# Attention steps of a two-layer decoder: the second scores of a key tile are issued ahead of the values of the tile before

## The reference: what is computed

```
w = jnp.einsum('bhnd,bhmd->bhnm', q, k) * jax.lax.rsqrt(float(D))
w = jnp.where(mask > 0, w, NEG)        # causal layers only
w = jax.nn.softmax(w, axis=-1)
attn = jnp.einsum('bhnm,bhmd->bhnd', w, v)
```

## Time and profile before

| | |
|---|---|
| median of 3 runs | 2826.07 us (2823.96 to 2826.38) |
| the profiled execution | 2821.3 us, its span 2819.5 us |
| PE busy | 2510.2 us, 89% |
| PE weight loads | 1440.7 us, 51% |
| DVE busy | 1492.1 us, 53% |
| ACT busy | 1328.4 us, 47% |
| POOL busy | 445.9 us, 16% |
| mean granted TensorE clock | 0.952 of full speed |
| context groups, 423 to 705 us | PE 266.5 us of 282, DVE 231.8, ACT 192.1, clock 0.99 |
| context groups, 1676 to 1930 us | PE 245.5 us of 254, DVE 206.5, ACT 175.1, clock 1.00 |

### The profile page before, as it was taken

One profiled execution on the slowest core, in us unless ns is written; L12 is line 12 of the kernel. 1 busy time (PEld: TensorE's weight loads), 2 busy tenths in 40 slices (PEclk: granted clock), 3 DMA queues, 4 the chain that ended last, 5 costly groups with the idle time before them and its releaser, 6 DMA issues. The chain is left out here.

```text
span 2819.5 us, 47227 instructions
## 1 busy us (share of the span) xinstructions
PE 2510.2 (89%) x15793; PEld 1440.7 (51%) x15794; DVE 1492.1 (53%) x4176; ACT 1328.4 (47%) x2833; POOL 445.9 (16%) x687
## 2 busy tenths in 40 slices
PE   6999999899979889998799999999998993599991
PEld 3555544444434456675466544444445653377661
DVE  2555877788544500023555688877746654222224
ACT  2655466667744422111355557666665551122220
POOL 4233221101100000000123312212023001400004
PEclk8999999999989999999799999999999995699996
DMA  7545533233000022113644543242223318201103
GB/s 222 162 142 144 139 98 94 53 80 79 1 1 0 1 95 95 63 49 120 196 128 141 144 98 94 53 116 71 66 86 98 101 44 292 96 30 33 33 30 95
DMA packets 153825, 259.89 MB, mean 92 GB/s; under 512 B 22713, under 2 KB 96705, under 8 KB 149441
## 3 DMA queue, kind: packets, MB, share of 16 engines
q1 hardware_dynamic: 150544, 248.81, 30.9%
q0 software_dynamic: 3072, 8.39, 0.9%
HBM read 180.71 MB, written 81.53 MB: 93 GB/s over the span
## 5 line engine op out<-in xcount | busy, mean ns | idle before, releaser
L1449 ACT ACTIVATE second_p<-psum 128x512 f32<-128x512 f32 (+3 forms) x1024 | 461.1, 522 | 234.7 <-PE psum L1291 231.2
L1449 ACT ACTIVATE first_p<-psum 128x512 f32<-128x512 f32 (+3 forms) x768 | 366.6, 548 | 164.2 <-PE psum L1291 160.8
L1541 DVE TENSOR_REDUCE second_max_parts<-psum 128x1 f32<-128x512 f32 x512 | 322.6, 683 | 67.6 <-PE psum L1268 65.5
L1541 DVE TENSOR_REDUCE first_max_parts<-psum 128x1 f32<-128x512 f32 x512 | 322.6, 683 | 63.3 <-PE psum L1268 61.0
L1537 DVE CUSTOM_DVE_ANT_0 second_masked<-psum,mask_qk 128x384 f32<-128x384 f32 (+3 forms) x512 | 229.4, 488 | 180.9 <-PE psum L1268 160.5
L1303 PE MATMUL psum<-second_p,second_v_aug 128*32 128x512 f32 (+3 forms) x2048 | 232.8, 527 | 6.0 <-ACT second_p L1449 4.8
L1268 PE MATMUL psum<-second_k,second_q 64*128 64x512 f32 (+3 forms) x1024 | 199.4, 386 | 28.3 <-DMA second_k<-a_k_parts 14.3
L1281 PE MATMUL psum<-second_q,second_k 64*128 64x512 f32 (+3 forms) x1024 | 222.1, 430 | 2.5 <-ACT second_shift_T L1460 0.7
L1291 PE MATMUL psum<-second_shift_T,choose 64*128 64x512 f32 (+3 forms) x1024 | 194.9, 376 | 0.0
L1281 PEld LDWEIGHTS psum<-second_q,second_k 64*128 64x128 f32 x1024 | 96.6, 184 | 182.1 <-ACT second_p L1449 76.5
L1303 PE MATMUL psum<-first_p,first_v_aug 128*32 128x512 f32 (+3 forms) x1536 | 184.9, 554 | 1.1 <-ACT first_p L1449 0.7
(11 more groups left out here) (337 smaller groups left out, 3867.5 us busy)
## 6 DMA issues: line engine op xcount, KB each, us to landing
first_k<-c_k_parts SPq DMA_DIRECT2D x64, 256.0 KB
second_q<-a_q_parts SPq DMA_DIRECT2D x128, 128.0 KB, 2.9
second_k<-a_k_parts SPq DMA_DIRECT2D x128, 128.0 KB, 2.9
second_k<-c_k_parts SPq DMA_DIRECT2D x64, 256.0 KB, 4.5
first_q<-a_q_parts SPq DMA_DIRECT2D x64, 128.0 KB
first_k<-a_k_parts SPq DMA_DIRECT2D x64, 128.0 KB
c_k_parts<-first_held SPq DMA_DIRECT2D x16, 512.0 KB, 3.1
first_q<-c_q_parts SPq DMA_DIRECT2D x64, 128.0 KB
```

What stands on the lines that cost most here:

```text
L1449: evacuated(act.activation(probs[tile % 2][:, 2 * h + p, q0:SEQ], bank[:, q0:SEQ], ACT.Exp, scale=scale), event)
L1541: evacuated(v.reduce_max(max_parts[n % 2][:, h, p, qt, k0 // BANK:k0 // BANK + 1], bank[:, 0:width], axis=AX_X), event)
```

## The change

The event scores (t,1), with the shift ahead of it in the last step, moves from behind the values, the turn and the loads to directly behind the first unit. The last two groups of each stage, which had it so already, stay as they are.

```diff
             share(units, 2 * t + 1, 2 * steps)
+            if n + 2 < groups:
+                if t == steps - 1:
+                    plan.append(("shift", n + 1, 0))
+                plan.append(("scores", n, (t, 1)))
             if t:
                 plan.append(("values", n, t - 1))
             elif n:
...
                 if n + 3 < groups:
                     plan.append(("vload", n + 3, 0))
-            if n + 2 < groups:
-                if t == steps - 1:
-                    plan.append(("shift", n + 1, 0))
-                plan.append(("scores", n, (t, 1)))
             share(units, 2 * t + 2, 2 * steps)
```

## The result

The changed kernel takes 2865.93 us (median of 4 runs, 2863.12 to 2869.14) against 2826.23 (4 runs, 2823.96 to 2830.89): 1.0137 times the time before, interval 1.0122 to 1.0152. It is slower by 39.7 us. The forecast was 2836, slower by 10.5, range 2812 to 2853. The direction was right, and so was the wait named as the one that takes the place of the removed one. The size was not, and a part that had been put at nothing, the steps with pieces, was not nothing. One of the twelve executions of the kernel with one-unit groups only took 6053.3 us and is left out of its ratio; every other execution in this document lies within 0.3% of its kernel's median.

What follows compares the result with a forecast made beforehand. ACT's latency loop binds plain context steps (2.94 us), DVE close behind. Terms -1 + 6.5 + 6 + 4 + 1 - 6 = +10.5 take the profiled 2821.3 to 2832, 2836 on the median's scale; range 2812 to 2853.

Steps and rivals of the forecast that it cites:

- Wait removed: Context steps: values stop waiting for ACT's second exponential, the first unit for the first; 0.34 us per plain step was waiting.
- Wait that takes its place: Plain context steps: second scores wait for DVE's maximum of the unit behind values; 2.93 against 2.94, 117 steps, -1 us.
- Turn: 25 context steps with the turn: the unit's maximum queues behind DVE's normalising multiply; +0.26 each, +6.5 us.
- shift: 23 context steps with the shift: second scores wait for both banks of the unit before; +0.26 each, +6 us.
- one unit: 10 steps with a single unit: no unit stands behind values, so DVE's wait can't arise; -0.6 each, -6 us.
- DVE's other work: 8 context groups with outputs: chain and statistics beyond DVE's spare 0.46 a step reach PE; 0 to +8, taken as +4 us.
- Causal groups without pieces: 12 groups: ACT-bound steps gain 2 x 0.34, the shift's wait for the chain loses 0.76; +1 us, bounds -8 to +9.
- Steps with pieces ...: 0: Steps with pieces (PE the bound), and groups 14 and 15 with four units a step (DVE the bound): no change, 0.
- the free wait: Rival, chance 0.12: DVE frees the bank by the time PE comes, all 0.34 a step is gained; 2764 us.
- weights loaded ahead: Rival, chance 0.08: the unit behind values starts as quickly as any, 0.12 x 165 = 20 less than forecast; 2816 us.
- plain exchange: Rival, chance 0.22: normalisation and double bank wait in turn and shift steps are hidden; -6, 2820 us.
- DVE becomes the bound: Rival, chance 0.18: in steps 0 to 2 and beside own pieces DVE's work passes 2.93 a step; +14, 2850 us.

Runs made afterwards that it cites:

- the kernel with one-unit groups only: Against the kernel before: second scores ahead of values only in the two groups whose steps have one unit; 2822.59 us, ratio 0.998.
- scores in pairs: Against the kernel before: in context groups both scores of a step in a row, then unit, values, unit; 2802.53 us, ratio 0.9904.
- The last step as before: The changed kernel, but a group's last step keeps the old order: values, shift, second scores; 2841.98 us, ratio 1.0055 to the kernel before.
- the halved maxima: DVE's maxima over context units read 256 of 512 columns: changed order 2804.25 us (0.9917), order before 2810.31 us (0.9937), ratios to the kernel before.

## Why the prediction was wrong

- *Wait removed:* right in sum. 6.0 us of idle before values of the second stage became 0.8. One reading was not shown: that the second exponential holds the values, 1.17 behind ACT's start. From the unit to the values are 0.46 before (1939.01 to 1939.47), and with scores in pairs, where ACT's exponentials were done before (it stood idle for 0.52 up to 531.92), still 0.44 (532.15 to 532.59). So the loop before may as well run through the unit's wait for the first exponential: 0.43 + 0.71 + 0.46 + 1.00 + 0.34 = 2.94. Both waits are ACT's, and the change removes both.
- *Wait that takes its place:* the right one, at the place named. Mis-sized: "a bank is free 0.73 after its maximum began" was read from maxima in a row. Behind an idle DVE it is 0.81 (544.77 to 545.58); behind the normalisation it is 0.73 again (2061.52 to 2062.25). The first maximum from idle lasts 0.69 where each in a row costs 0.60. With 0.04 from PE's late values start, less 0.02 in the two terms beside it, the step is 3.03 instead of 2.93: +9.9 in place of -1.
- *Turn, shift, one unit, DVE's other work:* right, each within 2 us. (The term for DVE's other work, +4, is compared with all context intervals with pieces, +3.3, which hold its statistics but not only them.)
- *Causal groups without pieces:* forecast +1, bounds -8 to +9, measured +8.4. In such a group the loss was priced at 0.76 and the gain at 0.68. Group 42 of stage "second" takes 2.16, 3.85, 2.60, 2.95 in its four steps before and 2.45, 3.27, 2.72, 3.46 after: the last step loses 0.51, the third 0.12, the first 0.29, and only the turn's step gains, 0.58. I had priced the shift's wait by the last step alone, while the unit of step 2 starts late as well and holds the chain. The 12 groups that were counted fit the 14 last steps behind no piece (+7.1 by the second cut); that steps without pieces stand in many other groups as well (68 intervals) was left out.
- *The step that failed is "Steps with pieces ...: 0".* It rested on one context step whose piece is bound by PE, and such steps did stay (+3.3 over 55, with the statistics). In causal groups the second scores of the last step, and then those of the next group's first step, lose the values as cover. Measured: 100 intervals, +14.5, of which some 5 are the slow-clock steps. By the second cut 7.4 of it stand in 28 last steps (0.46 each where ACT reads the piece twice, 0.14 each behind other pieces), and a group without a piece in its last step adds about 0.3 in the next first step. The last step as before removes the 7.4 to the last tenth.
- *The rivals:* the free wait and weights loaded ahead are refuted by 3.03 and by the 0.84 that still stands behind values, plain exchange by the turn and shift steps (3.73 and 3.53). "DVE becomes the bound" named the 0.08 that a maximum from idle costs, but as work; the halved maxima show latency.

Perfetto Trace Analysis of the Trainium skill, section "Optimization Strategy", says that a gap that repeats on the engine that should be busy can mean too few buffers. The trace agrees that the gap is a wait for a bank (0.49 before, 0.58 after); no run here has more banks, and an order alone took the wait away in context steps.

## What to carry to other kernels

When work is moved past a wait, list every consumer that it covered, in each kind of group apart, pieces and group ends too; an engine that is full beside a piece can still wait at its ends. When orders are compared, cut the traces where the same work lies between two cuts in both; a cut at the work that moved would have hidden here what the last step gives back. And look at the granted clock of each stretch before a difference is put down to the order. Take a release latency from rows where the releasing engine was idle, if it is idle in the new order. Where two latencies compete for one cover, place both of the long items so that each lies between a producer and the one who takes its bank: pairs of scores did this (2.94 to 2.71 a step), and moving the cover from one wait to the other did not.

## What the runs showed of the hardware

- A 128x512 maximum frees its bank 0.81 after its start from idle and 0.73 in a row or behind another instruction; with 256 columns 0.54.
- Small waits add: 0.08 of latency and 0.02 to 0.04 at the restart of PE, in 100 steps, are 10 us.
- The first matmul behind values (128x32 weights) took 0.49 to 0.51 instead of 0.39 wherever it had 512 columns, in every order run and in steps without units too; the weight load ahead of it stood idle for 0.84. A matmul whose bank comes late starts as slowly (0.51 at 532.15), as its weight load then starts with it.
- Eight matmuls (L1345, 128x256) took 1.97 at a granted clock of 1.00 and 3.65 at 0.53, in two kernels that differ only in order. Such spells fell on other steps from trace to trace, and one alone is worth 1.6 us.
